# Time mixing on other engines, and thirteen weight-turn groups in the expert choice

## The reference, cut to what matters

```
x = x + norm(time_mixing(norm(x)))
x = x + norm(expert_choice(norm(x)))
x = x + norm(delta_attention(norm(x)))
x = x + norm(mixture_of_experts(norm(x)))
```

```
xn = norm(x);  xl = norm(xn) * w + b          # its own first norm
r  = sigmoid(mix_r(xl) @ Wr.T);  k, v likewise without the sigmoid
den[t], num[t] = scans over the sequence in k and v
ratio = (e_prev * num + e_cur * v) / (e_prev * den + e_cur)
out = xn + (r * ratio) @ Wo.T
```

## Time and profile before

| | |
|---|---|
| median of 3 runs | 466.13 us (464.28 to 468.23) |
| span of the profiled execution | 468.2 us |
| PE busy | 345.0 us (74%) |
| DVE busy | 322.6 us (69%) |
| ACT busy | 256.0 us (55%) |
| POOL busy | 101.4 us (22%) |
| time mixing ends (last VectorE instruction) | 81.4 us |
| expert choice ends | 118.3 us |

### The profile page before, as it was taken

One profiled execution on the slowest core, in us unless ns is written; L12 is line 12 of the kernel. 1 busy time (PEld: TensorE's weight loads), 2 busy tenths in 40 slices (PEclk: granted clock), 3 DMA queues, 4 the chain that ended last, 5 costly groups with the idle time before them and its releaser, 6 DMA issues. The chain is left out here.

```text
span 468.2 us, 10194 instructions
## 1 busy us (share of the span) xinstructions
PE 345.0 (74%) x4018; PEld 270.8 (58%) x4018; DVE 322.6 (69%) x730; ACT 256.0 (55%) x527; POOL 101.4 (22%) x152
## 2 busy tenths in 40 slices
PE   1999778876599958252027788975999779888971
PEld 1544467765477747231026545654888677777861
DVE  5799997797416673999994368687895445542556
ACT  2879784466446782666223357657862336553241
POOL 6394000600000012200007400030077100003730
PEclk9999989897999997755559959997899789999986
DMA  7798000000000000000000000000012440222322
GB/s 217 243 353 294 0 0 1 0 2 0 0 3 1 3 3 1 0 1 1 0 0 3 4 3 6 3 1 1 1 45 102 132 162 1 91 104 88 99 60 90
DMA packets 18954, 24.84 MB, mean 53 GB/s; under 512 B 2582, under 2 KB 17068, under 8 KB 18860
## 3 DMA queue, kind: packets, MB, share of 16 engines
q1 hardware_dynamic: 17372, 19.99, 13.2%
q0 software_dynamic: 1536, 4.20, 2.8%
HBM read 18.02 MB, written 9.18 MB: 58 GB/s over the span
## 5 line engine op out<-in xcount | busy, mean ns | idle before, releaser
L1520 PE MATMUL ps<-ident,area 128*128 128x128 f32 x32 | 8.3, 409 | 40.6 <-DVE area L1850 40.6
L2198 PE MATMUL ps<-down_r,hidden_r 128*128 128x256 f32 x192 | 30.8, 320 | 6.7 <-DVE hidden_r L2498 3.8
L2198 PEld LDWEIGHTS ps<-down_r,hidden_r 128*128 128x128 f32 x192 | 29.4, 226 | 8.8 <-DVE hidden_r L2498 4.3
L2408 POOL DMA_INDIRECT stored<-results_dram,slots x16 | 16.7, 1045 | 67.4 <-DMA results_dram<-stored 62.8
L1520 PEld LDWEIGHTS ps<-ident,area 128*128 128x128 f32 x32 | 5.3, 202 | 43.4 <-DVE area L1850 43.4
L1847 DVE TENSOR_TENSOR third<-area 128x124 f32<-128x124 f32 (+15 forms) x31 | 29.3, 944 | 1.1
L1850 DVE TENSOR_TENSOR area<-area,third 128x124 f32<-128x124 f32 (+15 forms) x31 | 27.9, 901 | 1.1
L2230 PE MATMUL ps<-routed_up,xm_r 128*128 x138 | 23.4, 307 | 5.6 <-DVE stored L2510 2.7
L2182 PE MATMUL ps<-xm_r,gate_r 128*128 128x512 f32 x96 | 26.0, 407 | 1.0 <-ACT stored L2332 0.7
L1692 ACT ACTIVATE area<-ps,own_side 128x512 f32<-128x512 f32 (+1 forms) x16 | 15.9, 1100 | 19.1 <-PE ps L1520 19.1
L1748 ACT COPY area<-third 32x128 f32<-32x128 f32 x64 | 18.9, 295 | 13.1 <-DVE third L1894 11.9
(11 more groups left out here) (386 smaller groups left out, 987.4 us busy)
## 6 DMA issues: line engine op xcount, KB each, us to landing
stored<-in_L_ffn_sw_dram SPq DMA_DIRECT2D x3, 1024.0 KB
stored<-in_L_ffn_w_dram SPq DMA_DIRECT2D x1, 2048.0 KB
results_dram<-stored SPq DMA_DIRECT2D x2, 1024.0 KB, 4.5
stored<-rows_dram SPq DMA_DIRECT2D x1, 1920.0 KB, 8.0
x<-L_attn_hidden_state_dram SPq DMA_DIRECT2D x4, 256.0 KB, 3.6
out_dram<-x SPq DMA_DIRECT2D x4, 256.0 KB, 2.2
rows_dram<-L_attn_hidden_state_dram SPq DMA_DIRECT2D x1, 896.0 KB
stored<-rows_dram SPq DMA_DIRECT2D x1, 768.0 KB, 5.0
```

The lines of the kernel that those rows point to most:

```text
L1520: last = nc.tensor.transpose(ps[:, bank, i * P:(i + 1) * P], inv[:, r].rearrange("p q c -> p (q c)"), ident[:])
L2198: last = nc.tensor.matmul(ps[:, t // 2, t % 2 * D:(t % 2 + 1) * D], hidden_r[:, n % 2, hp, t * P:(t + 1) * P], down_r[:, wp, a, :], start= ...
L2408: nc.gpsimd.indirect_dma_start(found[:, k, t, :], None, core.results_dram, bass.IndirectOffsetOnAxis(slots[:, k, t:t + 1], 0)) \
```

## The change

Time mixing, all in the second half:
- Sequence 1's denominator and numerator: VectorE makes only the three products (`products`), and TensorE adds them by matmuls with the identity (`sum_second`), two for each of the two summands and each sum, 8 in all, into banks 2, 3 and 4, 5. ScalarE's Ln and VectorE's gate read the sums there. Sequence 0 is as before.
- The residual xn is put into banks 0 to 3 by identity matmuls (`add_rows`, 2 for each half) ahead of the projection, which accumulates on it. VectorE's add is gone, and its statistics read the banks.
- The norm of half 0 is applied by ScalarE from the banks (`normed(0)`), as half 1's, and GpSimd adds it to x, four adds of 128x256.
- `gated(1)` comes before the norm of half 0, and all statistics of the new x come at the end.
- Weight turns: 4, 3 and 4 groups through two banks (6 and 7) instead of 4, 9 and 6 through four.

The expert choice has 13 groups: two ahead of each of tiles 2 to 6, one ahead of tile 7, two behind it. ScalarE copies 3, 3, 3 and 4 behind the pairs of moments. The rest of the diff are counts of semaphores.

```diff
-        self.turned_early = (range(0, 4), range(4, 13), range(13, 19))
-        self.turned_late = range(19, len(self.all_tiles()))
-        self.turn_banks = range(4, 8)
+        self.turned_early = (range(0, 4), range(4, 7), range(7, 11))
+        self.turned_late = range(11, len(self.all_tiles()))
+        self.turn_banks = range(6, 8)
@@ time mixing, gpsimd
                 core.masks(pool, sem("masks_order"))
+                link = chain(pool, sem("masks_order"), core.pool_count)
+                for t in tiles_of[0]:
+                    pool.wait_ge(tail_normed, t + 1)
+                    link(nc.gpsimd.tensor_tensor(x[:, t], x[:, t], xl[:, t], ALU.add))
@@ time mixing, tensor
-                for b in range(B):
-                    core.turn_groups(pe, core.turned_early[b], core.turn_banks)
+                def add_rows(b):
+                    for t in tiles_of[b][::2]:
+                        nc.tensor.matmul(ps[:, t // 2, :], core.ident[:], xn[:, t:t + 2, :].rearrange("p t d -> p (t d)"),
+                                         start=True, stop=False, skip_group_check=True)
+
+                def project_out(b):
                     pe.wait_ge(rw_ready, b + 1)
-                    pe.wait_ge(v_kept, C * B)
                     for t in tiles_of[b]:
                         for c in range(C):
                             last = nc.tensor.matmul(ps[:, t // 2, (t % 2) * D:(t % 2 + 1) * D],
                                                     r[:, c, b, (t % TB) * P:(t % TB + 1) * P], w_t[:, OUT, c, :],
-                                                    start=c == 0, stop=c == C - 1)
+                                                    start=False, stop=c == C - 1, skip_group_check=True)
                         last.then_inc(rw_proj, 1)
-                core.turn_groups(pe, core.turned_early[B], core.turn_banks)
+
+                def sum_second(parts, bank):
+                    for n, part in enumerate(parts):
+                        for c in range(C):
+                            last = nc.tensor.matmul(ps[:, bank + c, :], core.ident[:], part[:, c, 1], start=n == 0,
+                                                    stop=n == len(parts) - 1)
+                    last.then_inc(proj, 1)
+
+                core.turn_groups(pe, core.turned_early[0], core.turn_banks)
+                pe.wait_ge(v_kept, C * B)
+                pe.wait_ge(xn_ready, NT)
+                add_rows(0)
+                project_out(0)
+                pe.wait_ge(den_ready, 2)
+                pe.wait_ge(cur_prev_exp, 2 * B)
+                sum_second((eb, ed), DEN_BANK)
+                pe.wait_ge(den_ready, 3)
+                sum_second((diff, mixed), NUM_BANK)
+                core.turn_groups(pe, core.turned_early[1], core.turn_banks)
+                pe.wait_ge(den_inverse, 3)
+                add_rows(1)
+                project_out(1)
+                core.turn_groups(pe, core.turned_early[2], core.turn_banks)
                 pe.wait_ge(sem("ffn_w_replaced"), core.turned_late[0])
@@ time mixing, scalar
                 core.keep_groups(act, core.turned_early[0], core.turn_banks)
-                invert(1)
-                core.keep_groups(act, core.turned_early[1][:3], core.turn_banks)
+                act.wait_ge(proj, SUMMED)
+                invert(1, ps[:, DEN_BANK:DEN_BANK + C, :])
+                core.keep_groups(act, core.turned_early[1], core.turn_banks)
+                def normed(b):
+                    act.wait_ge(tail_inverse, b + 1)
+                    for t in tiles_of[b]:
+                        norm.affine(out_rows, xl, t).then_inc(tail_normed, 1)
+
                 root(5, 0)
-                core.keep_groups(act, core.turned_early[1][3:], core.turn_banks)
+                normed(0)
                 core.keep_groups(act, core.turned_early[2], core.turn_banks)
                 root(6, 1)
-                act.wait_ge(tail_inverse, 1)
-                for t in tiles_of[1]:
-                    norm.affine(xn, xl, t).then_inc(tail_normed, 1)
+                normed(1)
@@ time mixing, vector
-                gated(0)
-                ratio(1)
-                residual(0)
-                gated(1)
-                link(outer_norm(0))
-                for t in tiles_of[0]:
+                gated(0, diff[:, :, 0])
+                products(1)
+                out_stats(0)
+                dve.wait_ge(proj, SUMMED + 1)
+                gated(1, ps[:, NUM_BANK:NUM_BANK + C, :])
+                outer_norm(0)
+                out_stats(1)
+                outer_norm(1)
+                for n, t in enumerate(tiles_of[0]):
+                    dve.wait_ge(sem("masks_order"), core.pool_count[0] - TB + n + 1)
                     after.tile_stats(x, t)
@@ expert choice, tensor
                 for n, t in enumerate(range(2, NT)):
-                    core.turn_groups(pe, core.turned_late[n:n + 1], LATE_BANKS)
+                    core.turn_groups(pe, core.turned_late[2 * n:min(2 * n + 2, len(core.turned_late) - 2)], LATE_BANKS)
                     experts(t)
+                core.turn_groups(pe, core.turned_late[-2:], LATE_BANKS)
@@ expert choice, scalar
-                    core.keep_groups(act, core.turned_late[2 * n:2 * n + 2], LATE_BANKS)
+                    core.keep_groups(act, core.turned_late[3 * n:3 * n + (3 if t < NT - 2 else 4)], LATE_BANKS)
```

More of the change, by code:

```diff
@@ L360, in time_mixing @@
         LN_W, LN_B, MIX_K, MIX_V, MIX_R, DECAY, BONUS = range(7)
+        out_rows = core.ps[:, 0:4, :].rearrange("p a (s d) -> p (a s) d", s=2)
+        DEN_BANK, NUM_BANK = 2, 4
+        SUMMED = 3 * C * B + 1
         BEFORE = -3.0e38
@@ L559, in _, with invert @@
                         .then_inc(xn_ready, 1)
-                def invert(b):
-                    act.wait_ge(den_ready, b + 1)
-                    a(ed[:, :, b], ed[:, :, b], ACT.Ln).then_inc(den_inverse, 1)
+                def invert(b, sums):
+                    a(ed[:, :, b], sums, ACT.Ln).then_inc(den_inverse, 1)
                     act.wait_ge(den_inverse, 2 * b + 1)
                     a(ed[:, :, b], ed[:, :, b], ACT.Exp, scale=-1.0).then_inc(den_inverse, 1)
-                invert(0)
+                act.wait_ge(den_ready, 1)
+                invert(0, ed[:, :, 0])
                 for b in range(B):
@@ L685, in ratio, with products, gated, out_stats @@
                     link(V.tensor_tensor(diff[:, :, b], diff[:, :, b], mixed[:, :, b], ALU.add))
-                def gated(b):
+                def products(b):
+                    dve.wait_ge(cur_prev_exp, 2 * b + 2)
+                    V.tensor_tensor(ed[:, :, b], ea[:, :, b], den[:, :, b, :T], ALU.mult).then_inc(den_ready, 1)
+                    V.tensor_tensor(diff[:, :, b], ea[:, :, b], num[:, :, b, :T], ALU.mult)
+                    V.tensor_tensor(mixed[:, :, b], eb[:, :, b], v[:, :, b], ALU.mult).then_inc(den_ready, 1)
+                def gated(b, sums):
                     dve.wait_ge(r_kept, C * (b + 1))
-                    link(V.tensor_tensor(r[:, :, b], r[:, :, b], diff[:, :, b], ALU.mult))
+                    link(V.tensor_tensor(r[:, :, b], r[:, :, b], sums, ALU.mult))
                     dve.wait_ge(den_inverse, 2 * b + 2)
                     V.tensor_tensor(r[:, :, b], r[:, :, b], ed[:, :, b], ALU.mult).then_inc(rw_ready, 1)
[L693 to L699, removed]
+                def out_stats(b):
+                    for t in tiles_of[b]:
+                        dve.wait_ge(rw_proj, (t // 2 + 1) * 2)
+                        last = norm.tile_stats(out_rows, t)
+                    link(last)
                     gather(b)
@@ L703, in outer_norm @@
                     inverse(norm.inv, 5 + b, b)
[L704 to L709, removed]
+                    norm.shift_by_mean(half_of[b]).then_inc(tail_inverse, 1)
                 for b in range(B):
@@ L715, in _ @@
                 scans(1)
-                gated(0)
-                ratio(1)
-                residual(0)
-                gated(1)
-                link(outer_norm(0))
-                for t in tiles_of[0]:
-                    after.tile_stats(x, t)
[L723 to L727, removed]
+                gated(0, diff[:, :, 0])
[8 more added lines that the diff above has]
+                    dve.wait_ge(sem("masks_order"), core.pool_count[0] - TB + n + 1)
+                    after.tile_stats(x, t)
+                for n, t in enumerate(tiles_of[1]):
+                    dve.wait_ge(tail_normed, TB + n + 1)
                     link(V.tensor_tensor(x[:, t], x[:, t], xl[:, t], ALU.add))
@@ L879, in _ @@
                 last.then_inc(limit_and_g, 1)
-                pe.wait_ge(sem("tail_normed"), TB + 1)
+                pe.wait_ge(sem("tail_normed"), NT + 1)
                 for n in range(STAY_WARM[1]):
@@ L932, in _ @@
                 norm.on_act(act, core.ln_eps[:])
-                act.wait_ge(sem("tail_inverse"), 2)
+                act.wait_ge(sem("tail_inverse"), B + 1)
                 for t in range(NT):
```

8 lines of the change are left out of this document (4 added, 4 removed).

## The result

The changed kernel took **473.3 us** (median of 4 runs, 472.17 to 474.25) against 465.6 for the kernel before, timed beside it: ratio **1.0148, 95% interval [1.0102, 1.0193]**, 7.7 us more by the medians. Ratios and intervals are estimated over the fast runs alone and aren't the quotient of the two medians (here 1.0165). The span of its profiled execution is 470.0 us; the time of an execution lies 2.1 to 2.2 us above its span.

A forecast was written before the change was run, and what follows sets the result against it. VectorE without gaps was taken to bound time mixing's second half; in the expert choice ScalarE's chain had 0.6 us to spare. Time mixing +1.9 and expert choice +7.0 gave 8.9 on the median 466.1: 475.0 us, range 472.5 to 477.5 (68%).

The forecast's parts named there:

- Sum and sign: Whole kernel: 1.9 us in time mixing plus 7.0 in the expert choice, 8.9 slower, 475.0 us; slower by over 1% given 0.82.
- Time mixing: Time mixing's second half: identity matmuls stand ahead of VectorE's gate, so the stage ends at 82.55 instead of 80.7, +1.9 us.
- the gate: Time mixing: VectorE waits until 67.6 for TensorE's sums, so its second gate ends at 70.1, against 67.97 before.
- second root: Time mixing, half 1's norm: ScalarE copies groups 7 to 10 until 77.15 and only then takes the root, to 77.5.
- pairs: End of time mixing: VectorE's four add-and-statistics pairs start at 79.3 and take 3.25 us as before.
- The clock in the second projection: Time mixing: second projection charged 3.55 us at full clock; a slow clock would make it 4.3, the stage 0.75 longer.
- GpSimd's adds: Time mixing, half 0's norm: four adds take 2.9 us, the lower bound; the upper was 10 us, ending the stage 3.2 later.
- The stepping through both queues: Expert choice: with two banks TensorE and ScalarE wait for each other in turn; ScalarE's copies end 7.55 us later, at 111.2.
- the root's slack of 0.6: Expert choice: ScalarE's root waited 0.61 us for VectorE before, so 7.55 us of delay costs 7.0.
- Later stages are the same: Stages behind the expert choice: no change in time, so no term in the sum.
- Interlock absent: Rival, 10%: orders slide past each other, only ScalarE's work counts; expert choice +0, time mixing +1.9, total 468.0 us.
- Only VectorE counts: Rival, 4%: time mixing loses VectorE's 7.9 us and the late groups hide; total 458.7 us, faster.

The follow-up runs named there:

- time mixing alone: The changed kernel with five late groups in the old order, the last eight weight groups left unturned: 469.1 us, ratio 1.0043 to the kernel before.
- the last version with five groups: Kernel before plus TensorE residual, half 0's norm on ScalarE and GpSimd, gate first, turns resplit, 34 warming transposes into an early-free bank: 461.2 us, ratio 0.9893.
- the order experiment: The changed kernel with two groups turned ahead of each of tiles 2 to 7, one behind, ScalarE copying 4, 4, 4, 1: 470.7 us, ratio 1.0075.
- the last two versions: Kernel before plus TensorE residual, half 0's norm moved, gate first: with 8 warming transposes 463.7, again 461.6 us; with 34 and other turn splits 461.2 us.

## Why the prediction was right or wrong

- **Sum and sign right**: 475.0 forecast, 473.3 and 474.5 measured, slower by over 1%. That the sum is this near is in part luck, as the points below say.
- **Time mixing right in its steps**: the gate 70.1 for 70.1, Ln 64.19 for 64.15, second root 77.31 for 77.15, pairs from 79.25 for 79.3, +1.8 for +1.9. Some 0.5 us of this closeness is luck: the execution of after stood 0.46 us later ahead of the first gate, and counted from that gate's end the change costs about 1.3. The cause was the one named: without the identity sums the same stage is 3.8 us shorter, counted so.
- **The clock in the second projection** was the right choice: 3.45 us, not 4.3, with TensorE busy ahead of it. This agrees with the rule in the Trainium skill, TensorE: Matmul & The Clock Gate, Part 1, that recent activity releases the clock.
- **GpSimd's adds** at the lower bound: 3.13 us for 2.9 forecast. The Trainium skill, GPSIMD Engine Reference, Key points, names as contending the VectorE instructions in a 2-port mode or with two SBUF inputs; the trace has none with two inputs beside these adds, and no run here shows the mode of those that it has.
- **The stepping through both queues right**: +7.75 for +7.55, with the two waits of over 2 us and the root's slack of 0.6 used up as forecast. The order that undoes the interlock shows it, but gives back 4.3 us of it and not all: the rest is TensorE's own work, which the prediction didn't set apart.
- **Wrong: "Later stages are the same", and no term for the way to the first pair.** The sum of 8.9 is near 7.7 by luck: two things that I had at nothing go against each other, 1.5 us for a longer stretch at half clock from the logits on, and, by the medians, 2 to 3 us that come back behind the root. I had looked for a cold clock only behind the expert choice. Whether the stretch is 3 or 6.5 us is not set by the late groups: time mixing alone had the short one (0.50 from 92.5 to 95.5), with the same code up to there as the changed kernel, the last version with five groups the long one. What sets it is open.
- **A rival was mis-sized.** "Interlock absent" had 468.0, from ScalarE's work alone. TensorE's own work, six tiles and thirteen groups, is longer: by the order experiment the expert choice would still be 3.5 us longer up to the centre, about 2.9 with the root's slack, so the rival's time was about 471.
- **Readings that were off without weight.** VectorE did have gaps in time mixing before the change, 1.06 us for a root at 76.39 and the 0.67 in the earlier trace rows at 77.43. The 468.2 is a span; that execution took about 470.3 us and was none of the three timed ones, whose slowest happened to take 468.23. The sum of "Only VectorE counts" is 466.1 less 7.9, or 458.2.

## What to carry to other kernels

Work moved into an engine's idle time must fit between its waits, not into their sum: step through both queues with the number of buffers, since two engines that hand over through two banks can wait for each other in turn, and another order of the same instructions may give much of it back (here 4.3 of 7.75 us). An operation moved off a busy engine helps only if its new way ends earlier; here 2.5 us of VectorE (five instructions that became three) turned into 6.9 us of TensorE (8 x 0.86) ahead of the same gate. Look at what a stage's end leaves for TensorE's clock in the next: of 4.9 and 4.5 us won in time mixing by the last two versions 2.0 and 3.0 were left at the next stage's root. And count a stage from a point ahead of the change, since two executions can differ there already, here by 0.46 us.

## What the runs showed of the hardware

In every profile of this study the granted clock fell to 1.2 GHz during the logits' matmuls (16 columns, TensorE busy 2.00 of 2.00 us from 88 to 90 in the kernel before) or within 1.6 us behind them, whether the stage before ended with 40, 36, 34 or 8 warming transposes. It stayed there for 3 to 3.5 us in some and 6.5 or more in others, each time the same in the three kernels that were profiled more than once. So a row that shows TensorE busy doesn't show that its clock will stay up; which property of these matmuls goes with the fall, no run sets apart. And code that is the same took 349.5 to 359.6 us from the root to the end in thirteen profiled executions, which is more than the whole effect of the change: medians over many runs and the stages' own rows had to be read side by side.
